# Moving an attention tile's output gate from VectorE to ScalarE and GpSimd

## The reference

```python
s   = attention(xn)         # chunked recurrence: 16 heads of width 8, then the output projection Wo
g   = silu(ffn(xn))         # 0.5 * shared experts + 0.5 * top-2 of 8 routed experts
out = x + s * g
```

## Time and profile before

| | us |
|---|---|
| median of 3 runs | 736.77 (736.12 to 741.37) |
| the profiled execution, its own time | 736.52 |
| its span, first to last instruction | 734.7 |
| TensorE matmul busy | 657.6 (90%) |
| VectorE busy | 575.1 (78%) |
| ScalarE busy | 484.7 (66%) |
| GpSimd busy | 454.7 (62%) |

### The profile page before, as it was taken

How to read it: one execution, slowest core, us unless ns; L and a number is a source line. 1 busy time by engine, 2 the same in 40 slices (tenths; PEclk the granted TensorE clock), 3 DMA queues, 4 the chain that set the end, 5 groups by cost and what they waited for, 6 DMA issues and landing times.

```text
span 734.7 us, 22308 instructions
## 1 busy us (share of the span) xinstructions
PE 657.6 (90%) x8520; PEld 457.7 (62%) x8520; DVE 575.1 (78%) x1095; ACT 484.7 (66%) x985; POOL 454.7 (62%) x490
## 2 busy tenths in 40 slices
PE   2677787997999999999999999999997899999993
PEld 1444465665666665566666667788895667666672
DVE  6989997987677886667676667666764899999996
ACT  5865578684666666566666666666665677877772
POOL 2434322225777777777777777677777566666763
PEclk9999999998999999999999999999999999999997
DMA  9931112101111232433323334323444757767642
GB/s 243 278 101 44 44 44 86 60 3 35 45 45 51 95 102 90 151 109 105 105 95 109 104 105 151 99 96 106 105 109 119 216 197 230 230 200 212 209 138 58
DMA packets 88616, 86.75 MB, mean 118 GB/s; under 512 B 11394, under 2 KB 65284, under 8 KB 88516
## 3 DMA queue, kind: packets, MB, share of 16 engines
q1 hardware_dynamic: 79428, 66.70, 29.1%
q0 software_dynamic: 9088, 18.63, 9.7%
HBM read 50.82 MB, written 34.47 MB: 116 GB/s over the span
## 4 chain that ended last, share of the span: by engine, by line
PE 43%; DVE 30%; issue 9%; POOL 8%; ACT 6%; DMA 3%; SPq 0%; DVEq 0%; ACTq 0%; POOLq 0%
PE banks L1509 7%; PE banks L1510 7%; PE banks L1511 7%; DVE wwords L1259 7%; DVE hidden L1276 6%; DVE hidden L1174 5%; PE banks L1549 5%; POOL expert_rows L629 4%; PE banks L1529 4%; PE banks L1530 4%; PE banks L1528 4%; POOL srows L619 3%; ACT hidden L747 2%; ACT hidden L743 2%; DMA srows<-normed_rows,source 2%
## 5 line engine op out<-in xcount | busy, mean ns | idle before, releaser
L747 ACT CAST hidden<-hidden 128x512 f16<-128x512 f32 x206 | 127.2, 618 | 144.1 <-DVE hidden L1174 144.0
L1178 DVE TENSOR_TENSOR hidden<-hidden 128x512 f16<-128x512 f32 x178 | 122.9, 691 | 82.4 <-ACT hidden L747 81.4
L619 POOL DMA_INDIRECT srows<-normed_rows,source x142 | 148.8, 1048 | 54.0 <-issue 40.5
L1174 DVE TENSOR_TENSOR hidden<-hidden,banks 128x512 f32<-128x512 f32 x206 | 140.7, 683 | 42.4 <-ACT hidden L743 37.1
L1528 PE MATMUL banks<-wwords,hidden 128*128 (+1 forms) x824 | 149.8, 220 | 1.4 <-DVE hidden L1178 1.0
L1530 PE MATMUL banks<-wwords,hidden 128*128 (+1 forms) x824 | 149.7, 220 | 0.0
L1529 PE MATMUL banks<-wwords,hidden 128*128 (+1 forms) x824 | 149.7, 220 | 0.0
L743 ACT ACTIVATE hidden<-banks 128x512 f32<-128x512 f32 x206 | 122.8, 596 | 27.9 <-PE banks L1511 27.7
L1509 PE MATMUL banks<-sx,wwords 128*128 128x512 f16 (+1 forms) x368 | 121.5, 330 | 0.6 <-DVE sx L1167 0.6
L1511 PE MATMUL banks<-sx,wwords 128*128 128x512 f16 (+1 forms) x368 | 121.6, 330 | 0.0
L1510 PE MATMUL banks<-sx,wwords 128*128 128x512 f16 (+1 forms) x368 | 121.5, 330 | 0.0
(11 more groups left out here) (213 smaller groups left out, 1416.0 us busy)
## 6 DMA issues: line engine op xcount, KB each, us to landing
rows<-x SPq DMA_DIRECT2D x32, 256.0 KB, 5.2
rows<-expert_rows SPq DMA_DIRECT2D x32, 256.0 KB, 3.4
normed_rows<-rows SPq DMA_DIRECT2D x16, 256.0 KB, 3.9
r_rows<-rows SPq DMA_DIRECT2D x16, 256.0 KB, 2.1
rd_rows<-rows SPq DMA_DIRECT2D x16, 256.0 KB, 2.0
stage<-r_rows SPq DMA_DIRECT2D x16, 256.0 KB, 5.4
k_rows<-rows SPq DMA_DIRECT2D x16, 256.0 KB, 2.1
kd_rows<-rows SPq DMA_DIRECT2D x16, 256.0 KB, 2.1
```

What stands on the lines that cost most here:

```text
L619: G.indirect_dma_start(srows[:, q % NXB, t, :], None, rows_in, bass.IndirectOffsetOnAxis(source[:, at:at + 1], 0)).then_inc(sem[f"s_in{q % ...
L747: A.copy(guh[:, i % 4, :], gu[:, i % 2, :]).then_inc(sem["gu_hi"], 1)
L1174: V.tensor_tensor(gu[:, i % 2, :], sg[:, i % 2, :], psum[2 * (i % 2) + 1][:, :], ALU.mult).then_inc(sem["gated"], 1)
```

## The change

The gate of tiles 0 to 13 is split. ScalarE copies the scaled output product from PSUM bank 1 into `res` (`act_out(u-2)`, between `act_weigh(u-1,0)` and `act_kv(u,0)`). GpSimd multiplies `res` with the expert rows (`pool_gate(u-1)`) and then adds x as before (`pool_end(u-1)`). In GpSimd's round `pool_mask(2(u+1)+1)`, which stood after `pool_end`, now stands ahead of both. TensorE's `pe_update` waits for ScalarE's copy where it waited for the gate, and SyncE loads the next expert rows after GpSimd's multiplication. Tiles 14 and 15 keep VectorE's gate.

```diff
@@ sp_moe
                 if u >= PRING:
-                    nc.sync.wait_ge(sem["s_read"], u - PRING + 1)
+                    nc.sync.wait_ge(sem["gated_out"], u - PRING + 1)
@@ gpsimd
+            def pool_gate(u):
+                s = u % 2
+                G.wait_ge(sem["out_read"], u + 1)
+                G.wait_ge(sem["moe_silu"], u + 1)
+                G.tensor_tensor(res[:, s, :], res[:, s, :], picked[0][:, u % PRING, :, :].rearrange("p b d -> p (b d)"),
+                                ALU.mult).then_inc(sem["gated_out"], 1)
+
             def pool_end(u):
                 s = u % 2
-                G.wait_ge(sem["s_read"], u + 1)
+                if u < NA - 2:
+                    G.wait_ge(sem["gated_out"], u + 1)
+                else:
+                    G.wait_ge(sem["s_read"], 1)
@@ gpsimd, loop over u
                 if at(u):
                     pool_add(u, 0)
                     pool_add(u, 1)
+                if at(u + 1):
+                    pool_mask(2 * (u + 1) + 1)
+                if at(u - 1) and u - 1 < NA - 2:
+                    pool_gate(u - 1)
                 if at(u - 1) and u - 1 < NA - 1:
                     pool_end(u - 1)
-                if at(u + 1):
-                    pool_mask(2 * (u + 1) + 1)
@@ scalar
+            def act_out(u):
+                A.wait_ge(sem["s_out"], u + 1)
+                if u >= 2:
+                    A.wait_ge(sem[f"stored{u % 2}"], 16 * (u // 2))
+                A.mul(res[:, u % 2, :], psum[1], 1.0 / SY / SW).then_inc(sem["out_read"], 1)
@@ scalar, loop over u
                 if at(u - 1):
                     act_weigh(u - 1, 0)
+                if at(u - 2) and u - 2 < NA - 2:
+                    act_out(u - 2)
                 if at(u):
                     act_kv(u, 0)
@@ vector, loop over u
-                if at(u) and u < NA - 2:
-                    dve_gate(u)
@@ pe_update
                 if u >= 2:
-                    T.wait_ge(sem["s_read"], u - 1)
+                    T.wait_ge(sem["out_read"], u - 1)
```

## The result

The changed kernel takes 757.78 us (median, 754.59 to 761.40) where the kernel before takes 738.17 (736.12 to 741.37) in the same comparison: 1.027 times as long, 95% interval 1.023 to 1.031. The forecast was 756.1, with a range of 751 to 764. The profiled execution took 754.59 us with a span of 752.8; before, 736.52 and 734.7. The span grew by 18.1 us.

A forecast was written before the change was run, and what follows sets the result against it. VectorE at 9.80 us a round, with a ring through GpSimd, TensorE and ScalarE at 9.74, bound the kernel; 734.7 + 19.0 + 0.3 = 754.0 span, with 1.8 outside 755.8, median 0.25 higher: 756.1 us, range 751 to 764.

The forecast's parts named there:

- What bounds the kernel: Kernel before, one round: VectorE full at 9.80 us, with a wait loop through the other engines only 0.06 us shorter.
- VectorE's ring: VectorE's own 15 instructions per round with nothing between them: 9.80 us, of which the gate takes 0.59.
- the second ring: Loop of waits from state step through GpSimd's mask and low halves, TensorE and ScalarE back to state step: 9.74 us.
- the free time: GpSimd's idle time between the mask and the second low half: 1.07 us a round was free for added work.
- VectorE's gate gives back 0.06 a round: VectorE loses 0.59 us of work a round, but only 0.06 comes back, since the second ring is late next.
- GpSimd's chain behind the mask: Gate and residual, 2.59 us, delay the second low half to 4.46 us after the state step; round 11.26, loss 1.46.
- ScalarE's copy costs nothing here: ScalarE's 0.59 us copy out of PSUM runs while TensorE computes k and v for 1.25 us; taken as nothing.
- the second rival: Order on GpSimd costs nothing, ScalarE's place decides: 736.0, or 743.1 with the copy on the second ring; chance 0.07.
- SyncE and the stores cost nothing: Expert-row loads come about 4.7 us later, and the copy into `res` waits for an earlier store; both costed at nothing.
- Count and tail: Thirteen rounds at 1.46 us give 19.0 us; the fourteenth delays only the last output projection, 0.3 us more.
- TensorE's stalls would add to both kernels: TensorE's two short stalls in this stretch belong to the second ring before and after the change, so they add to both.
- The clock: Rival: TensorE's granted clock falls to 0.83 from idling, 1.2 us more a round, 772 us; chance 0.05.

## Why the prediction was right, point by point

*What bounds the kernel.* Right in size: VectorE's ring of 9.80 us and one of 9.74 right behind it. Without the gate the round measured 9.75. But the path of the second ring was misread, and only luck kept that out of the numbers. Three rows of TensorE in the undisturbed round without the gate, whose state steps are at 609.29 and 619.04:

```profile
611.87 1.10 PE L1649 MATMUL banks<-wwords 64*32 64x256 f32 x32 [0.55 <-DVE hidden L1283]
612.98 0.23 PE L1660 MATMUL banks<-brw,f2y 128*128 128x128 f16 x1
617.23 1.09 PE L1649 MATMUL banks<-wwords 64*32 64x256 f32 x32
```

TensorE waits for VectorE's selection (L1283 there), does the first half's scores times values, and from there on has no idle time up to the state products: 2.58 us from the state step, 1.11, and 6.06 from the projection to the next state step are 9.75, through VectorE and TensorE alone. The second low half, which waits for ScalarE's high half (1.02 us) and not for the mask, comes at 612.24, and with its 0.73 it is ready at 612.97, at the very moment at which TensorE gets there. ScalarE's copies of k and v hide behind TensorE's own work too: the 0.94 and the 0.91 us from copy to matmuls in the earlier trace rows are the scores (1.05 us) and the second half's scores times values (1.02). GpSimd's chain thus tied with TensorE's, and any delay of it beyond the free time counted in full, as the prediction had it.

*VectorE's gate gives back 0.06 a round.* Right, 0.05. The rule of the Trainium skill, page Perfetto Trace Analysis, section Optimizing Scalar/DVE Operations, that a saturated DVE may justify moving work away, has its condition fulfilled here and yields nothing measurable in that run (0.9966 to 1.0004 of the kernel before): being full and being the only bound are two things.

*GpSimd's chain behind the mask.* Right in mechanism and size. Multiplication and residual took 1.36 + 1.24 = 2.60 us from start to start (forecast 2.59), the second low half came 4.47 us after the state step (4.46; the first is at 636.21, its successor 0.63 later, the state step at 632.37), and the round was 11.24 (11.26). Undoing the order alone brought back 9.74 to 9.79, and the order without the multiplication cost 0.08. The spans in GpSimd's rows, 1.28 + 1.28, give 2.56: the Trainium skill's page Perfetto Trace Analysis, section GPSIMD Engine Instruction, which wants starts compared, agrees: by the spans 0.04 us would be missing.

*ScalarE's copy costs nothing here.* Right, since it runs under k and v. The statement beside it, that in the round as it was the copy would lengthen the ring by 0.4 to 0.59, and with it the second rival's 10.29, was wrong: I took the 0.94 us from copy to matmuls for a latency, while TensorE was doing scores in them. Measured, the copy comes 0.24 late and costs nothing.

*SyncE and the stores cost nothing.* Right: no engine waited for a transfer in the rounds.

*Count and tail.* 13 rounds, as forecast: 13 x (11.24 - 9.80) = 18.7. The tail took 0.50 for the 0.3 forecast. That TensorE's stalls would add to both kernels was wrong: the kernel before has 1.2 us of them in two rounds, and in the changed one they vanish in the wait of 1.52 us. Against that stands the slow round, 1.50 us; the two offset each other, and that they do is luck. Most of the 1.2 us between the forecast span of 754.0 and the 752.8 measured is the 1.05 us ahead of these rounds, which the change doesn't touch.

*The clock.* I gave it 0.05, as a fall for every round to 0.83. It does fall, but in one round of thirteen in one execution and four in another, and each costs 1.5 to 1.6 us rather than 1.2. My evidence against it, a wait of 1.5 us at 577 us that left the clock alone, was one case of a thing that goes either way.

## What to carry to other kernels

A full engine is worth relieving only by as much as the next ring of waits is shorter; here that was 0.06 us, and walking the ring through the timelines gave it before any run. The next ring can run through the same engine: a different order of VectorE's own instructions, with no work less, gave 0.25 us a round where leaving out its gate gave 0.05. An engine's idle time has a place: work added between a step that starts late and the step that others wait for costs its whole length beyond the free time at that very spot, so put it behind the last thing that others wait for. And a distance between two rows is a latency only if the second engine had nothing else to do in it; a step belongs to the ring only where a row shows that it was waited for.

## What the runs showed of the hardware

TensorE's clock can fall after a short wait. Two rounds of the changed kernel, each with the stretch around the wait and the one behind it:

```profile
622.20:624.80 2.60, 1.10 (x32) 0.56 (x32) 2.60 (x4) 2.60 (x9) 2.57 (x4) 0.97 0.53 155
624.80:628.35 3.55, 3.52 (x33) 3.30 (x33) 1.76 (x4) 1.13 (x3) 3.16 (x3) 0.54 1.02 276
...
635.00:637.50 2.50, 1.05 (x32) 0.50 (x32) 2.50 (x4) 2.50 (x9) 2.50 (x4) 1.00 0.50 149
637.57:641.00 3.43, 3.43 (x69) 2.83 (x70) 1.92 (x5) 1.69 (x4) 3.14 (x3) 1.00 1.02 282
```

In both TensorE did the same 32 matmuls and then stood for 1.52 us. After the first the granted clock was 0.54 in the mean over the next 3.55 us, so mostly at the lower level, 1.2 GHz; after the second it stayed at 1.00. Over the two executions of this kernel that were profiled it fell in 5 of 26 rounds. In four of the 26 the wait was only 0.79 to 1.19 us, since a stall had come before it, and in these the clock stayed at 1.00. With a wait of 2.50 us it fell in 13 of 13, and with matmuls of no use in the wait in none of the 13 rounds in each of three executions (in two of these it fell once ahead of them, where the recurrence begins, after stalls of 1.79 and 2.18 us). A fall costs 1.4 to 1.6 us here. It is also a likely part of the changed kernel's spread: its four executions in the first comparison ran from 754.59 us at a mean clock of 0.983 to 761.40 at 0.976. That share wasn't measured by itself.

What TensorE's stalls without a releaser are, up to 1.3 us each in the rounds and at places that differ from kernel to kernel, stays open. One candidate is untested: the profile has a DMA queue for instructions, and a transfer of it lies in the microsecond or two ahead of the stalls of 1.14 us (without the gate, transfer in 648 to 649, stall from 649.31) and of 1.30 us (gate one tile later, 706 to 708, stall from 707.54). But such transfers come every 4 to 5 us in the rounds without a stall as well. Open is also why two of the three chips need some 100 us more for the experts' part.
